# Sums of weights by accumulating transfers, and token columns held by pair, in a Flamingo-style gated block on one core

## The reference

```python
x = x + tanh(g_xattn[0]) * xattn(layernorm(x), ctx)      # 32 query heads, 8 key/value heads of 128
x = x + tanh(g_ffn[0]) * ffn(layernorm(x))
# xattn: q = rmsnorm(h @ Wq.T), k = rmsnorm(ctx @ Wk.T), v = ctx @ Wv.T
#        softmax(q k^T / sqrt(128) + mask) v, then @ Wo.T
# ffn:   scores = h @ Wr.T; gates = softmax of the 16 largest of 64 experts
#        out = sum over experts of ((h @ A_k.T) * gate_k) @ B_k.T, times 2
```

## Time and profile before

| | before |
|---|---|
| median of runs | 2540.8 us |
| profiled execution, its time | 2547.66 us |
| its span, first to last instruction | 2545.8 us |
| PE / DVE / ACT / POOL busy | 91% / 66% / 46% / 59% |
| mean granted TensorE clock | 0.965 of 2.4 GHz |
| moved by DMA | 427.69 MB, mean 168 GB/s |
| packets | 329770, 238704 of them under 2 KB |

### The profile page before, as it was taken

One profiled execution on the slowest core, in us unless ns is written; L12 is line 12 of the kernel. 1 busy time (PEld: TensorE's weight loads), 2 busy tenths in 40 slices (PEclk: granted clock), 3 DMA queues, 4 the chain that ended last, 5 costly groups with the idle time before them and its releaser, 6 DMA issues.

```text
span 2545.8 us, 35745 instructions
## 1 busy us (share of the span) xinstructions
PE 2323.6 (91%) x11384; PEld 1929.5 (76%) x11384; DVE 1680.2 (66%) x2631; ACT 1178.5 (46%) x3731; POOL 1511.4 (59%) x2134
## 2 busy tenths in 40 slices
PE   5998996999999989999999799999998998878899
PEld 4886884888777778887888688788787876666687
DVE  6656556777677787766777835755757877454755
ACT  4545554556565676655666722322324234232321
POOL 6877557777677767766765344644655665334431
PEclk8999998999999999999999799999999998989899
DMA  4767565444444464444432544546455578564753
GB/s 175 252 200 256 157 219 170 121 133 132 130 133 129 120 224 133 133 133 133 133 104 86 182 160 152 198 156 211 162 166 199 182 215 273 148 227 128 242 174 140
DMA packets 329770, 427.69 MB, mean 168 GB/s; under 512 B 16240, under 2 KB 238704, under 8 KB 317552
## 3 DMA queue, kind: packets, MB, share of 16 engines
q1 hardware_dynamic: 329584, 425.39, 52.3%
HBM read 275.91 MB, written 149.42 MB: 167 GB/s over the span
## 4 chain that ended last, share of the span: by engine, by line
PE 41%; POOL 24%; DMA 20%; issue 7%; DVE 5%; SPq 2%; ACT 1%; POOLq 0%; ACTq 0%; DVEq 0%
PE bank L773 13%; PE bank L775 13%; PE bank L774 13%; DMA mini_combo<-in_sets 9%; DMA combos<-mini_combo 4%; POOL s_hi L1730 4%; POOL staged L1720 2%; POOL staged L1724 2%; POOL staged L1718 2%; DVE s_lo L1276 2%; POOL mini_combo L1808 2%; DMA gates_of_ranks<-gates_t 2%; POOL mini_combo L1805 1%; POOL mini_combo L1810 1%; POOL mini_combo L1806 1%
## 5 line engine op out<-in xcount | busy, mean ns | idle before, releaser
L773 PE MATMUL bank<-t_hi,s_hi 128*128 128x512 f32 x2720 | 1116.4, 410 | 120.6 <-DVE s_lo L1276 50.1
L775 PE MATMUL bank<-t_hi,s_lo 128*128 128x512 f32 x2720 | 1081.4, 398 | 0.0
L774 PE MATMUL bank<-t_lo,s_hi 128*128 128x512 f32 x2720 | 1080.0, 397 | 0.0
L1276 DVE TENSOR_TENSOR s_lo<-staged,s_hi 128x512 fp32r<-128x512 f32 x676 | 571.1, 888 | 211.8 <-ACT s_hi L1007 148.6
L773 PEld LDWEIGHTS bank<-t_hi,s_hi 128*128 128x128 f32 x2720 | 523.5, 192 | 236.8 <-issue 85.7
L775 PEld LDWEIGHTS bank<-t_hi,s_lo 128*128 128x128 f32 x2720 | 522.0, 192 | 116.2
L774 PEld LDWEIGHTS bank<-t_lo,s_hi 128*128 128x128 f32 x2720 | 524.7, 193 | 94.8
L1007 ACT CAST s_hi<-staged 128x512 fp32r<-128x512 f32 x452 | 260.5, 622 | 428.8 <-DMA staged<-heads 194.8
L1718 POOL TENSOR_TENSOR staged<-staged 128x512 f32<-128x512 f32 x96 | 136.4, 1421 | 305.7 <-DMA staged<-gated 104.3
L1386 DVE SCALAR_TENSOR_TENSOR probs<-bank,small,mask 128x128 f32<-128x128 f32 x512 | 144.0, 343 | 163.3 <-POOL small L1710 109.1
L1101 ACT ACTIVATE probs<-probs,small 128x128 f32<-128x128 f32 x512 | 198.0, 387 | 53.5 <-DVE small L1390 52.5
(11 more groups left out here) (124 smaller groups left out, 3225.8 us busy)
## 6 DMA issues: line engine op xcount, KB each, us to landing
heads<-heads SPq DMA_DIRECT2D x128, 256.0 KB, 3.7
t_raw<-combos SPq DMA_DIRECT2D x24, 1024.0 KB, 9.0
staged<-in_w_q SPq DMA_DIRECT2D x32, 768.0 KB, 5.7
staged<-heads SPq DMA_DIRECT2D x32, 768.0 KB, 5.9
t_raw<-in_sets SPq DMA_DIRECT2D x22, 1024.0 KB, 8.8
mini_combo<-in_sets SPq DMA_DIRECT2D x80, 256.0 KB, 3.4
combos<-mini_combo SPq DMA_DIRECT2D x80, 256.0 KB, 2.3
sums<-sums SPq DMA_DIRECT2D x18, 1024.0 KB, 7.9
```

Of the source, the lines that this page charges most:

```text
L773: nc.tensor.matmul(out[:, :], s_hi[w][:, cols], t_hi[k][:, at, :], start=start, stop=False, skip_group_check=True)
L774: nc.tensor.matmul(out[:, :], s_hi[w][:, cols], t_lo[k][:, at, :], start=False, stop=False, skip_group_check=True)
L775: done = nc.tensor.matmul(out[:, :], s_lo[w][:, cols], t_hi[k][:, at, :], start=False, stop=at == 3, skip_group_check=True)
L1276: return nc.vector.tensor_tensor(out, whole, hi.bitcast(FP32), ALU.subtract)
```

## The change

What it does:

- The small and the 1 MB load-compute-store pieces go, with their buffers. For each of the sets 1 to 6 SP now copies blocks in DRAM (two DMAs of 2 MB, `combo_copies`), and POOL then issues three accumulating DMAs in DRAM (2 MB, 1 MB, 1 MB, `combos`), each after the one before has landed. Step 0 (the copies) to step 3 lie in four following entries: 1 to 4 for set 1, and n = 2 to 23 without 15 and 16 for the sets 2 to 6 (copies at n = 2, 6, 10, 14 and 20). The first set's steps are at SP's j = 5 and POOL's j = 4, the others' at SP's r = 3, behind all else, and POOL's r = 2, behind `sums`.
- The block sums change in sign, so that all of them are additions in DRAM; the signs of the stationary sums, of the token columns' sums and of the results' sums change to match. The number and shapes of those operations stay.
- Token columns are laid out as `[set, k, pair, partition, 512]`: one store per pair of 1.75 MB in runs of 2 KB instead of seven. The reload reads four runs of 2 KB per partition, and PE's moving operand in the four token sets is four runs of 128 columns, 512 apart.

```diff
@@ Declared
-        self.xt = scratch("xt", 2, 7, P, 4, 4, S)
-        self.x2t = scratch("x2t", 2, 7, P, 4, 4, S)
+        self.xt = scratch("xt", 2, 7, 4, P, HALF)
+        self.x2t = scratch("x2t", 2, 7, 4, P, HALF)
@@ program
-    MINI_SLOTS = [(n, r) for n in range(32) if n not in (15, 31) for r in (0, 1, 3)][:80]
-    mini_at = {slot: u for u, slot in enumerate(MINI_SLOTS)}
+    def combo_steps(e):
+        if 1 <= e <= 4:
+            return [(1, e - 1)]
+        return [(2 + u // 4, u % 4) for u, n in enumerate(n for n in range(2, 24) if n not in (15, 16)) if e == QA0 + n]
@@ refill
-                if k == 0 and which == 1:
-                    sp.wait_ge(pc_out, 64)
-                elif k == 0:
-                    sp.wait_ge(mc_out, 256 * (which - 1))
+                if k == 0:
+                    sp.wait_ge(combo_added, 48 * which)
@@ sync
+        def combo_copies(e):
+            for which, step in combo_steps(e):
+                if step == 0:
+                    if which > 1:
+                        sp.wait_ge(combo_added, 48 * (which - 1))
+                    sums, raw = d.combos[which].rearrange("b p c -> p b c"), d.sets[which].rearrange("b p c -> p b c")
+                    sp.dma_start(sums[:, 0:2, :], raw[:, 0:2, :]).then_inc(combo_copied, 16)
+                    sp.dma_start(sums[:, 2:4, :], raw[:, 0:4:2, :]).then_inc(combo_copied, 16)
@@ columns_out (finish likewise, with x2t)
-            for k in SEVEN:
-                sp.dma_start(d.xt[u // 4, k, :, :, u % 4, :], xo[:, k, :, :]).then_inc(xt_out, 16)
+            sp.dma_start(d.xt[u // 4, :, u % 4].rearrange("k p c -> p k c"), xo[:, :, :, :].rearrange("p k b q -> p k (b q)")).then_inc(xt_out, 16)
@@ part
+            if entry.tau in TOKEN_SETS:
+                out = out.rearrange("p (a c) -> p a c", a=4)
+                high = t_hi[k][:, :, at * P:at * P + P]
+                low = t_lo[k][:, :, at * P:at * P + P]
@@ gpsimd
+        def combos(e):
+            for which, step in combo_steps(e):
+                sums, raw = d.combos[which], d.sets[which]
+                if step == 0:
+                    continue
+                if step == 1:
+                    pool.wait_ge(combo_copied, 32 * which)
+                    to, part = sums[2:4].rearrange("b p c -> p b c"), raw[2:4].rearrange("b p c -> p b c")
+                if step == 2:
+                    pool.wait_ge(combo_added, 48 * which - 32)
+                    to, part = sums[0], sums[3]
+                if step == 3:
+                    pool.wait_ge(combo_added, 48 * which - 16)
+                    to, part = sums[1], sums[0]
+                nc.gpsimd.dma_start(to, part, accum_op=ALU.add, max_dma_last_dim=8192).then_inc(combo_added, 16)
```

More of the change, by code:

```diff
@@ L58 @@
 TAUS = 11
+TOKEN_SETS = (2, 3, 8, 9)
 FILL_POSITIONS = (4, 5, 6, 7, 9, 10, 11)
@@ L269, in program @@
     pc_at = m.at
-    pc = m.put("combo", [P, 4, HALF])
+    m.put("b21_room", [P, 4, HALF])
     xr = [m.put(f"x_rows{w}", [P, HIDDEN]) for w in range(2)]
@@ L577, in finish @@
                     sp.wait_ge(fo_pool, 2 * f + 2)
[L578 to L590, removed]
+                    sp.dma_start(d.x2t[p // 4, :, p % 4].rearrange("k p c -> p k c"),
+                                 xo2[:, :, :, :].rearrange("p k b q -> p k (b q)")).then_inc(ft_out, 16)
         def gate_rows_in(r):
@@ L671, in _ @@
                     values_out(e, 0)
-                    if combo_unit(e + 1) is not None and e < 15:
-                        combo_in(combo_unit(e + 1), pc)
+                    combo_copies(e)
                 if j == 6 and e and e % 2 == 0:
@@ L701, in _ @@
                     keys_out(15, 1)
[L702 to L705, removed]
+                if r == 3:
+                    combo_copies(e)
         heads_out(127)
@@ L772, in part @@
             start = k < 4 and at == 0
-            nc.tensor.matmul(out[:, :], s_hi[w][:, cols], t_hi[k][:, at, :], start=start, stop=False, skip_group_check=True)
-            nc.tensor.matmul(out[:, :], s_hi[w][:, cols], t_lo[k][:, at, :], start=False, stop=False, skip_group_check=True)
-            done = nc.tensor.matmul(out[:, :], s_lo[w][:, cols], t_hi[k][:, at, :], start=False, stop=at == 3, skip_group_check=True)
+            out, high, low = out[:, :], t_hi[k][:, at, :], t_lo[k][:, at, :]
+            if entry.tau in TOKEN_SETS:
+                out = out.rearrange("p (a c) -> p a c", a=4)
+                high = t_hi[k][:, :, at * P:at * P + P]
+                low = t_lo[k][:, :, at * P:at * P + P]
+            nc.tensor.matmul(out, s_hi[w][:, cols], high, start=start, stop=False, skip_group_check=True)
+            nc.tensor.matmul(out, s_hi[w][:, cols], low, start=False, stop=False, skip_group_check=True)
+            done = nc.tensor.matmul(out, s_lo[w][:, cols], high, start=False, stop=at == 3, skip_group_check=True)
             if at == 3:
@@ L1290, in plus, with minus, from_bank @@
             return nc.vector.tensor_tensor(out, a, bank[BANK_OF[k]][:, :], ALU.add).then_inc(taken[BANK_OF[k]], 1)
+        def minus(out, a, k):
+            return nc.vector.tensor_tensor(out, a, bank[BANK_OF[k]][:, :], ALU.subtract).then_inc(taken[BANK_OF[k]], 1)
+        def from_bank(out, k, a):
+            return nc.vector.tensor_tensor(out, bank[BANK_OF[k]][:, :], a, ALU.subtract).then_inc(taken[BANK_OF[k]], 1)
         def second_product(e):
@@ L1826, in _ @@
         pool.wait_ge(t0_combo_pool, 1)
-        nc.gpsimd.tensor_tensor(t_raw[6][:, :, :], b21_again[:, :, :], t_raw[1][:, :, :], ALU.subtract).then_inc(t0_combo_pool, 1)
+        nc.gpsimd.tensor_tensor(t_raw[6][:, :, :], b21_again[:, :, :], t_raw[1][:, :, :], ALU.add).then_inc(t0_combo_pool, 1)
         for e in range(KV0, QA0):
             for j in SEVEN:
-                if j == 1 and combo_unit(e) is not None:
-                    combos(combo_unit(e), pc)
+                if j == 4:
+                    combos(e)
                 if j == 2 and e:
@@ L1862, in _ @@
                     values_high(n - 1)
-                if (n, r) in mini_at:
-                    mini(mini_at[n, r])
+                if r == 2:
+                    combos(e)
         for e in range(O0, A0):
```

97 lines of the change are left out of this document (27 added, 70 removed).

## The result

| | before | after |
|---|---|---|
| median of runs | 2540.8 us | 2449.8 us |
| ratio, 95% interval | | 0.9639 (0.9623 to 0.9656) |
| profiled execution: its time, span | 2547.7, 2545.8 | 2446.7, 2444.7 |

The change makes the kernel 91 us, 3.6%, faster.

The account below looks back on a forecast made before the run. The loop of small loads, four POOL operations and stores was taken to set the pace. Gains 68.5 + 12 + 1 + 5 = 86.5 less costs 12 + 5 = 17, net -70 from 2540.8, gave 2471 us; range 2440 to 2530.

Parts of the forecast that it names:

- rival D: Whole kernel: costs are nil and clock dips go with the stalls, 2440 to 2455 us; chance 0.09.
- (1): Attention stage, 26 entries: without the small load-compute-store loop they fall to 29.31 us each; gain 68.5 us.
- (2): Entry before those 26, 428.47 to 473.98 us: PE's 11.4 us wait for the softmax goes; gain 12, between 6 and 16.
- (3): Key/value stage, second operand set's sums: POOL's lost time lies beside PE; gain 1 us, at most 3.
- (6): DRAM copies, 4 MB per set: 2 us each, 10 in the attention stage and 2 before; cost 12 us.
- (4): Column stores, seven per pair made one: about a quarter of ScalarE's 18.1 us router-stage waits reaches PE; gain 5, 0 to 12.
- (5): Token-set matmuls, PE's moving operand in four runs: cost taken as 0, range 0 to 41 us.
- Rival C: Token-set matmuls: four runs cost PE 5 ns each, 17 us, giving 2488 us; chance 0.08.
- (7): Accumulating transfers issued by POOL, three per set, 18 in all: 0.3 us each, cost 5 us.
- Rival A: Attention stage: accumulations delay the values' loads and POOL, giving back half the gain, 2505 us; chance 0.20.
- Rival B: Slow accumulation makes POOL wait: gain gone at 39.6 us per 2 MB, 2603 us at 50; chance 0.12.
- Rival E: Attention stage: the loop is not the pace, entries keep 32 us; 2523 to 2540, 2530 taken; chance 0.05.

Follow-up runs that it names:

- the kernel with a quarter of the work: The kernel before with one of POOL's four operations on each small piece, all transfers and waits kept: 2465.9 us, ratio 0.9699.
- the sums' part alone: The kernel after with its columns put back (seven stores, 512-byte runs), keeping the accumulating transfers: 2466.1 us, ratio 0.9719.
- the columns' part alone: The kernel before with only one store per pair, 2 KB runs and the moving operand in four runs: 2530.2 us, ratio 0.9961.
- the three kernels with a part of the loop: The kernel before with POOL's operations but only the first small load; all transfers without operations; one operation in four: 2462.0, 2462.3, 2465.9 us.
- POOL's pieces and the single stores: The kernel after with the second operand set's sums made as before (1 MB loads, four POOL operations, stores): 2446.7 us, ratio 0.962.
- The spare accumulations: The kernel after with an extra accumulation into an unread block in each of 22 attention entries: 2554.8 us with 2 MB, 2479.2 with 1 MB.

## Why the prediction was right, point by point

It forecast 2471, the time is 2449.8, in the range. The direction and the mechanism were right; the gain was 91 us, not 70, and the range held it because it reached down to rival D. Counted in traces the forecast was 70 and the gain 101, in its own terms: the middle of the stage 53.5 (68.5 less 15 of costs) against 66.5, the head 12 against 26.3, the second set -1 against -6.0, the stores 5 against 7.0, and 7.3 us in places that no term covers (entries 8, 9, 50 and the rest).

- **(1), the middle of the attention stage, 68.5:** measured 66.5. The floor of 29.31 us per entry was read from three entries that already ran without the loop, and the 26 entries now take it; the 7.8 us left in for the change of operand stayed to 0.01 us, and the entry after it keeps 1.8 us more, which is most of the difference of 2. The path as I told it (what waits behind POOL's waits is late) was too narrow here: the experiments show that POOL's waits and work together filled it. One sign of being right was not met: DVE still waits 38.3 us for `small`, not under 20, and PE does not feel it.
- **(2), the head of the stage, 12:** the path was right, the size was not. PE's wait of 11.4 us is gone (0.2 now), the clock of the stretch went from 0.85 to 1.00, and by the kernel with a quarter of the work it is POOL's wait that makes PE's. Entry 18 gained 16.7, more than the upper bound of 16, the entries 16 and 17 another 9.5 that stood in no sum. Small pieces run from n = 0 on, and I read only the entry with the 11.4 us wait. In the sums' part alone entry 17 takes 22.4 us for 28.8, in the columns' part alone 29.3, and in the three kernels with a part of the loop 21.4 to 24.0: it is POOL's loop there too. Of the 3.1 us of entry 16 none came with the sums' part alone (34.4 us) and 2.2 with the columns' part alone, as far as one trace each can tell.
- **(3) and (6), the second set, +1 - 2:** -6.0. That POOL's time lies beside PE there was right: with POOL's pieces and the single stores the entries 2 to 6 lose 0.1 us in all. But a 2 MB accumulation in front of a stationary load stood in no term. In the attention stage that load is issued 13 us behind it and landed after 5.8 to 6.6 us, which nothing waited long for; here it comes 9 us behind it, with a column store between.
- **(4), the stores, 5:** 7.0 in entries 77 to 81, for another reason than told: in those entries the run length, not the number of issues, and not by ScalarE's wait of 18.1 us in the router stage.
- **(5), four runs, 0:** right. The last three entries on such an operand take 87.92 us in both kernels, and the matmuls on it follow each other by 0.22 to 0.24 us (603.73, 603.96, 604.20, 604.42, 604.66), as in one run. Rival C is out.
- **(6) and (7), costs of 17:** each pair of copies had landed 16.0 to 18.0 us after its first issue, just within the 18 us from which it would hold anything up, and cost nothing to be seen in the attention stage; nor did the accumulations, though POOL's issue took 0.9 to 1.2 us and not 0.4. The whole cost of 15 in that stage was too careful.
- **Rival A** is real and was small: POOL waits 18.6 us, six times, for values (those issued 5.4 us behind a 2 MB accumulation landed after 9.2 to 10.0 us), and PE does not feel it, because POOL has 265.6 us to spare. The spare accumulations show the price when it grows. **Rival B** needed 39.6 us for 2 MB; it takes 13.9. **Rival D** (2440 to 2455) is where the time lies, with the clock at 1.00 for 0.99 and 0.85 in the stretches of the earlier trace rows. **Rival E** is out: DMA share rose from 0.45 to 0.53 and the entries got shorter.
- The rule of the Trainium skill (SBUF — State Buffer, SBUF: two separate sides) that GpSimd's descriptors wait while VectorE runs a two-port operation has no row here. The 18 issues took 0.83 to 1.36 us, and no run tells a wait for descriptors from the transfer itself.

## What to carry to other kernels

Look in the same trace for a stretch that already runs without what you want to remove; its pace is a better forecast than any sum of what goes. For an engine that executes in order add its work and its waits against the length of the entry: where the sum is only just too long, removing either can be enough. Look at single entries as well, because where one long wait stands in front of something urgent, as in entry 18, less work does not help. When work moves from an engine to transfers, ask for each step which short transfer is issued next and how many microseconds later: the same 2 MB accumulation was free with 13 us of distance to the next stationary load and cost 8 us with 9 and a column store between.

## What the runs showed of the hardware that I had not expected

- Accumulating in DRAM takes some 1.6 times as long as copying: 2 MB landed after 13.9 us in the median, 7 us per MB, and pairs of copies, 4 MB, within 16.0 to 18.0 us, 4.0 to 4.5 per MB.
- A moving operand in four runs of 128 columns costs PE nothing: 518 instructions of PE in 87.92 us either way.
- The price of extra accumulating traffic grew: 1.3 us for each of the first 22 MB over the stage, 3.4 for each of the next 22.
